# A decoder layer on one core: the third LayerNorm, the router and the transfers into expert order moved into the LSTM recurrence

## The reference

```
x = x + attention(layernorm(x))                       # 16 heads of 8, one shared K and V
x = x + xattn(layernorm(x), context)                  # two-layer LSTM with attention, 64 steps
x = x + ffn(layernorm(x))                             # eight experts, one per token

def step((h0, c0, h1, c1, a), x_t):                   # 64 times, each needs the one before
    h0, c0 = lstm([x_t, a], h0, c0);  h1, c1 = lstm(h0, h1, c1)
    p = softmax((h1 @ Wq.T) . context[b])             # over the 64 context rows of b
    a = tanh([p @ context[b], h1] @ Wo.T + bo);  return a

logits = x @ router_W + router_b                      # ffn, on x = layernorm(...)
gates = one_hot(argmax(softmax(logits))) * softmax(logits)
y = relu(x @ W1[e] + b1[e]) @ W2[e] + b2[e];  out = gates . y
```

## Time and profile before

| | us |
|---|---|
| median of 3 runs | 1802.16 (1801.74 to 1804.47) |
| profiled execution | 1804.93, span 1803.2 |
| TensorE busy | 1479.9 (82%), weight loads 1289.7 (72%) |
| VectorE busy | 1159.9 (64%) |
| ScalarE busy | 736.0 (41%) |
| POOL busy | 220.0 (12%) |

### The profile page before, as it was taken

How to read it: one execution, slowest core, us unless ns; L and a number is a source line. 1 busy time by engine, 2 the same in 40 slices (tenths; PEclk the granted TensorE clock), 3 DMA queues, 4 the chain that set the end, 5 groups by cost and what they waited for, 6 DMA issues and landing times. The chain is left out here.

```text
span 1803.2 us, 82779 instructions
## 1 busy us (share of the span) xinstructions
PE 1479.9 (82%) x34347; PEld 1289.7 (72%) x34348; DVE 1159.9 (64%) x4481; ACT 736.0 (41%) x1856; POOL 220.0 (12%) x427
## 2 busy tenths in 40 slices
PE   1547777777756999999999999999999968249997
PEld 0436666666645888888888888888888858237665
DVE  5878888888875666565656566666666658425454
ACT  2436666665643344444434343434443422013332
POOL 0000000000000000000000000000000003743333
PEclk9868988888966999999999999999999975569999
DMA  6000000000030000000000000000000036322221
GB/s 222 1 1 1 0 0 0 0 0 0 0 84 12 1 0 0 0 0 0 0 0 0 0 0 0 0 0 0 0 0 0 0 103 208 128 84 75 75 75 42
DMA packets 33458, 50.04 MB, mean 28 GB/s; under 512 B 4714, under 2 KB 24684, under 8 KB 32648
## 3 DMA queue, kind: packets, MB, share of 16 engines
q1 hardware_dynamic: 27312, 35.50, 6.7%
q0 software_dynamic: 5376, 12.66, 2.0%
q10 hardware_dynamic: 728, 1.34, 0.2%
HBM read 30.52 MB, written 19.48 MB: 28 GB/s over the span
## 5 line engine op out<-in xcount | busy, mean ns | idle before, releaser
L1554 DVE TENSOR_TENSOR hb<-psH,b_sb 128x512 f32<-128x512 f32 x72 | 49.8, 692 | 118.4 <-PE psH L1349 118.4
L891 PE MATMUL sc_a<-h_a,KH 128*128 128x48 f16 (+2 forms) x4096 | 123.9, 183 | 2.5 <-DVE h_a L1045 2.5
L891 PE MATMUL sc_b<-h_b,KH 128*128 128x48 f16 (+2 forms) x4096 | 122.9, 183 | 0.0
L851 PE MATMUL z_a<-h_a,WL 128*128 128x64 f16 x2304 | 112.5, 193 | 9.3 <-DVE h_a L1037 1.9
L851 PE MATMUL z_b<-h_b,WL 128*128 128x64 f16 x2304 | 111.9, 193 | 8.4 <-DVE h_b L1037 0.6
L931 PEld LDWEIGHTS mx_b<-pmv_b,VH 128*128 128x128 f16 x4096 | 107.1, 96 | 16.4 <-DVE pmv_b L1073 16.4
L931 PEld LDWEIGHTS mx_a<-pmv_a,VH 128*128 128x128 f16 x4096 | 107.1, 96 | 16.2 <-DVE pmv_a L1073 16.2
L931 PE MATMUL mx_b<-pmv_b,VH 128*128 128x16 f16 x4096 | 113.0, 169 | 5.4 <-DVE pmv_b L1073 0.4
L931 PE MATMUL mx_a<-pmv_a,VH 128*128 128x16 f16 x4096 | 113.0, 169 | 5.2 <-DVE pmv_a L1073 0.4
L891 PEld LDWEIGHTS sc_a<-h_a,KH 128*128 128x128 f16 x4096 | 112.8, 96 | 2.8 <-DVE h_a L1045 2.6
L466 PE MATMUL psK<-ident,xn 128*128 128x128 f32 x64 | 20.9, 327 | 113.2 <-DVE VB L671 86.6
(11 more groups left out here) (291 smaller groups left out, 3556.6 us busy)
## 6 DMA issues: line engine op xcount, KB each, us to landing
xr<-sorted_x SPq DMA_DIRECT2D x72, 129.0 KB, 2.1
XT<-in_ctxT SPq DMA_DIRECT2D x1, 4096.0 KB, 13.2
x_scratch<-X SPq DMA_DIRECT2D x1, 4096.0 KB, 15.9
TOK<-x_scratch SPq DMA_DIRECT2D x4, 1024.0 KB, 10.6
sorted_x<-zt SPq DMA_DIRECT2D x16, 129.0 KB, 6.4
w_sb<-in_w SPq DMA_DIRECT2D x1, 2048.0 KB, 10.3
b_sb<-in_b SPq DMA_DIRECT2D x1, 2048.0 KB, 21.1
out<-ys,xr POOLq DMA_INDIRECT x72, 2.3
```

The source lines that it names most:

```text
L851: mm = nc.tensor.matmul(q.z[layer][:, j * GB:(j + 1) * GB], WL[:, blk + j, w, :], mov[m], start=False, stop=False, skip_group_check=True)
L891: mm = nc.tensor.matmul(A.S[:, WIDE * n:WIDE * n + streamed(n)], KH[:, k, pair * P:(pair + 1) * P], A.h[1][:, 2 * n:2 * n + streamed(n) // ...
L1554: nc.vector.tensor_tensor(hb[:, u, :], psH[:, u, :], b1_sb[:, bass.ds(col, FF)], ALU.add).then_inc(v_hb, 1)
```

## The change

The hand-over up to `tables` is taken out of block 5 and put into block 4, one token tile per step, as a pipeline of which each stage runs a step or half a step behind the one before. n is the tile, t the step; `odd` is the group whose attention part runs in this half (0: a, 1: b).
- Half 0 of step t: TensorE transposes a of tile t-1 (both groups, now side by side in `A32`) and does `routing` (logits of t-3, ranks of t-4); VectorE normalises t-2, makes the gate of t-4 and adds x1 of t-1; ScalarE copies logits and ranks; POOL copies the normalised x of t-2 and the row numbers into `TOK`.
- Half 1: TensorE transposes the normalised x of t-2; VectorE does the statistics of t-1 and the maximum of the logits of t-3; ScalarE copies the transposed x and does the exponential; POOL does `place` of t-4, `rstd` of t-1 (a reciprocal root by three rounds of Newton), `choose` of t-3, and the indirect transfer of t-4.
- Four steps T to T+3 without recurrence drain the pipeline; then one matmul gives the totals and `tables` runs.
- ScalarE, POOL and VectorE loop over four steps a turn, and eight first and four last steps are written out.
- The two groups share one bank for the scores and one for the mixture; the two banks that this frees, `psE` and `psF`, carry the new matmuls.
- x1 comes by one load per tile; W1 and W2 are loaded into `X`, b1 beside it, all during the recurrence. The copies of a32 to X go. In the diff below the order is TensorE, VectorE, ScalarE, POOL; `place` and `choose` are 5 and 7 instructions of one to eight columns, written like those of `rstd`. Block 5 loads only b2 and runs the tile loop, which is unchanged.

```diff
-                q.a32 = sb(f"a32_{t}", [P, GB])
+                q.a32 = A32[:, g * GB:(g + 1) * GB]
-                q.S = ps("sc")
-                q.M = ps("mx")
+                q.S = psS
+                q.M = psM
...
+            def run_steps(eng, first_half, step, turn):
+                first_half()
+                for t in range(HEAD):
+                    step(t, t % SLOTS)
+                with eng.Fori(HEAD, T - TAIL - turn + 1, turn) as t:
+                    for k in range(turn):
+                        step(t + k, (HEAD + k) % SLOTS)
+                for t in range(T - TAIL, T + 4):
+                    step(t, t % SLOTS)
...
+                    def turn_a(n):
+                        pe.wait_ge(G[0].s_ta, n + 1)
+                        pe.wait_ge(G[1].s_ta, n + 1)
+                        wait(pe, a_xt, n - 1)
+                        nc.tensor.transpose(psE[:, 0:P], A32[:, :], ident[:, :]).then_inc(p_e1, 1)
+                    def turn_xn(n):
+                        pe.wait_ge(v_xn, n + 1)
+                        pe.wait_ge(v_x2, n + 2) if live(n + 1) else None
+                        nc.tensor.transpose(psE[:, 0:P], XN[:, :], ident[:, :]).then_inc(p_e2, 1)
+                    def routing(t):
+                        if live(t - 3):
+                            pe.wait_ge(a_xt, t - 2)
+                        if live(t - 4):
+                            pe.wait_ge(g_one, t - 3)
+                            wait(pe, g_acc, t - 4)
+                        wait(pe, a_lr, t - 3)
+                        if live(t - 3):
+                            nc.tensor.matmul(psF[:, 0:NE], xT[:, :], rw_sb[:, :], start=True, stop=False)
+                            mm = nc.tensor.matmul(psF[:, 0:NE], ones[0:NE, :], rbd[:, :], start=False, stop=True)
+                        if live(t - 4):
+                            nc.tensor.matmul(psF[:, NE:2 * NE], upper[:, :], one[:, :], start=True, stop=False)
+                            mm = nc.tensor.matmul(psF[:, NE:2 * NE], ones16[:, :], acc[:, :], start=False, stop=True)
...
                             if not last:
                                 early1(A)
+                        if odd == 0 and live(t - 1):
+                            turn_a(t - 1)
+                        if odd == 1 and live(t - 2):
+                            turn_xn(t - 2)
...
+                        if odd == 0:
+                            routing(t)
+                        if A:
                             pe.wait_ge(A.s_pm, 2 * at + 2)
...
+                        if odd == 0:
+                            if live(t - 2):
+                                normalise(t - 2, (m - 2) % SLOTS)
+                            if live(t - 4):
+                                gate(t - 4, (m - 4) % SLOTS)
+                        if odd == 1:
+                            if live(t - 1):
+                                statistics(t - 1, (m - 1) % SLOTS)
+                            if live(t - 3):
+                                best(t - 3)
                         if A:
                             dve.wait_ge(A.s_sc, at + 1)
...
+                        if odd == 0 and live(t - 1):
+                            add_x1(t - 1, (m - 1) % SLOTS)
...
+                        if odd == 1 and live(t - 2):
+                            act.wait_ge(p_e2, t - 1)
+                            wait(act, p_lr, t - 2)
+                            nc.scalar.activation(xT[:, :], psE[:, 0:P], ACT.Copy).then_inc(a_xt, 1)
+                        if odd == 1 and live(t - 3):
+                            act.wait_ge(v_nm, t - 2)
+                            nc.scalar.activation(eg[:, :], lr[:, 0, :], ACT.Exp, bias=nm[:, 0:1],
+                                                 accum_out=sm[:, 0:1]).then_inc(a_eg, 1)
...
+                    def after(n):
+                        pool.wait_ge(g_r, n)
+                        pool.sem_inc(g_go, 1)
+                    def rstd(n):
+                        ready(v_ag, n + 1)
+                        ready(v_xn, n)
+                        k = 11 * n
+                        pool.tensor_scalar(ve[:, :], mv[:, 1:2], EPS, None, ALU.add).then_inc(g_r, 1)
+                        after(k + 1)
+                        pool.tensor_scalar(yr[:, :].bitcast(I32), ve[:, :].bitcast(I32), -0.5, 1597463007.0,
+                                           ALU.mult, ALU.add).then_inc(g_r, 1)
+                        pool.tensor_scalar(vh[:, :], ve[:, :], -0.5, None, ALU.mult).then_inc(g_r, 1)
+                        for i in range(3):
+                            after(k + 3 * i + 3)
+                            pool.tensor_tensor(yu[:, :], yr[:, :], yr[:, :], ALU.mult).then_inc(g_r, 1)
+                            after(k + 3 * i + 4)
+                            pool.tensor_scalar(yu[:, :], yu[:, :], vh[:, 0:1], 1.5, ALU.mult, ALU.add).then_inc(g_r, 1)
+                            after(k + 3 * i + 5)
+                            if i < 2:
+                                pool.tensor_tensor(yr[:, :], yr[:, :], yu[:, :], ALU.mult).then_inc(g_r, 1)
+                            else:
+                                pool.tensor_tensor(rs[:, :], yr[:, :], yu[:, :], ALU.mult).then_inc(g_rs, 1)
...
+                        if odd == 0 and live(t - 2):
+                            copy_xn(t - 2, (m - 2) % SLOTS)
+                        if odd == 1:
+                            if live(t - 4):
+                                place(t - 4, (m - 4) % SLOTS)
+                            if live(t - 1):
+                                rstd(t - 1)
+                            if live(t - 3):
+                                choose(t - 3)
+                            if live(t - 4):
+                                scatter(t - 4, (m - 4) % SLOTS)
-                            pool.tensor_copy(X[:, bass.ds(at * B + A.g * GB, GB)], A.a32[:, :]).then_inc(A.s_ao, 1)
```

More of the change, by code:

```diff
@@ new lines, in decoder_kernel @@
+            z2 = sb("z2", [P, 2])
+            z1 = sb("z1", [P, 1])
+            one = sb("one", [P, NE], F16)
+            acc = sb("acc", [P, NE], F16)
+            w8 = sb("w8", [P, NE])
+            w4 = sb("w4", [P, 4])
+            w2s = sb("w2s", [P, 2])
+            slot = sb("slot", [P, SLOTS], U32)
+            zt = sb("zt", [P, ROW])
+            base = sb("base", [P, NE])
+            first = sb("first", [P, NE])
+            cnt = sb("cnt", [P, NE])
+            cnti = sb("cnti", [P, NE], I32)
@@ new lines, in decoder_kernel @@
+            unit = sb("unit", [P, NE])
+            end = sb("end", [P, NE])
+            tilestart = sb("tilestart", [P, NT])
+            past = sb("past", [P, NT, NE])
+            tex = sb("tex", [P, NT])
+            rowf = sb("rowf", [P, NT])
+            lasti = sb("lasti", [P, NE], I32)
+            d_x1 = [sem(f"d_x1{u}") for u in range(SLOTS)]
+            d_sc = [sem(f"d_sc{u}") for u in range(SLOTS)]
+            d_rw = sem("d_rw")
+            d_w = sem("d_w")
+            d_z = sem("d_z")
@@ new lines, in decoder_kernel, with live @@
+            a_lr = sem("a_lr")
+            a_eg = sem("a_eg4")
+            g_c = sem("g_c4")
+            g_go = sem("g_go4")
+            g_r = sem("g_r")
+            g_rs = sem("g_rs")
+            g_xn = sem("g_xn")
+            g_pl = sem("g_pl")
+            g_acc = sem("g_acc")
+            g_one = sem("g_one")
+            g_ch = sem("g_ch")
+            def live(n):
+                return not isinstance(n, int) or 0 <= n < T
+            def run_steps(eng, first_half, step, turn):
[7 more added lines that the diff above has]
+                    step(t, t % SLOTS)
@@ new lines, in run_halves, with step @@
+            def run_halves(half, eng, turn):
+                def step(t, m):
+                    if not isinstance(t, int) or t < T - 1:
+                        half(G[1], G[0], t, t, t, m)
+                        half(G[0], G[1], t + 1, t, t, m)
+                    elif t == T - 1:
+                        half(G[1], G[0], t, t, t, m)
+                        half(None, G[1], None, t, t, m)
+                    else:
+                        half(None, None, None, None, t, m, 0)
+                        half(None, None, None, None, t, m, 1)
+                run_steps(eng, lambda: half(G[0], None, 0, None, None, None, None), step, turn)
@@ L939, in _, with half @@
                         early1(q)
-                    run_halves(half, pe)
+                    run_halves(half, pe, 1)
+                    pe.wait_ge(g_acc, T)
+                    pe.wait_ge(a_lr, T + 1)
+                    nc.tensor.matmul(psF[:, 0:NE], ones16[:, :], acc[:, :], start=True, stop=True).then_inc(p_lr, 1)
                 @block.scalar
                 def _(act):
-                    def half(L, A, lt, at):
+                    def half(L, A, lt, at, t, m, odd=-1):
+                        odd = A.g if A else odd
                         def gate_tanh(l):
@@ new lines, in half @@
```

(16 more changed lines are left out.)

508 lines of the change are left out of this document (211 added, 297 removed).

## The result

The changed kernel takes 1898.7 us (median of four runs, 1896.3 to 1968.1) against 1803.1 before: ratio 1.0529, interval 1.0511 to 1.0547. It is slower by 96 us. The forecast was 1742 us. The run of 1968.1 had a granted clock of 0.63 throughout, so the profile shown here is that of a later run of 1899.5 us. It belongs to a group of runs in which the kernel before takes 1823.3 and the changed one 1903.8, ratio 1.0431 (1.0375 to 1.0488).

The account below looks back on a forecast made before the run. TensorE, hardly resting, was taken to bound the recurrence, and POOL's work the hand-over. 1804.93 - 89.6 (hand-over) + 27 (steps) + 3 (start) = 1745.3, less 2.8 for the runs' median: 1742.5 us, range 1715 to 1795.

Parts of the forecast that it names:

- What comes into each step: Part of the prediction pricing the work added to each recurrence step, engine by engine: 0.42 us a step, 27 us over 64.
- `add_x1` (an operation like `sm`, 0.29) lies in the 0.42 ahead of `pmv`: VectorE in the recurrence step: the added 0.29 us operation fits in the 0.42 us VectorE waits before `pmv`.
- without a wait for pmv: Sign in the half with `routing`: weight loads of `mx` start about 0.3 us later after WO's, with no wait for `pmv`.
- POOL as the bound: POOL in the recurrence step: bound only above 0.44 us an instruction; over 0.5 was included in a rival of chance 0.12.
- 24 x 0.28 ... = 10.1 of 13.9: POOL in the recurrence step: 24 small instructions at 0.28 us, copies and a scatter take 10.1 of 13.9 us.
- The hand-over: Between recurrence and tile loop: 128.8 us goes, 39.2 stands in its place, so 89.6 us is given back.
- The start: Before TensorE's first matmul: some twenty small POOL instructions and the router weights' load add 2 to 4 us, taken as 3.
- The shared banks: PSUM banks of scores and mixture, shared by both groups in the recurrence: no wait is added, 0.
- The sum on TensorE: Recurrence step: TensorE gets 0.70 us more work, 0.30 of it on the path for `routing`; all additions together 0.42.
- Rival 1: Recurrence step: TensorE absorbs nothing, all 0.70 us added plus 0.15 of late `sm`, 54 us in all, 1769.5 us; chance 0.20.
- rival 2: Recurrence step: everything hides but 0.1 us a step, 6 us in place of 27, 1721.5 us; chance 0.08.
- Rival 3: Recurrence: POOL's activity stretches VectorE's two-SBUF-input operations, deciding from 0.93 us a step; 1838 us at three per half; chance 0.12.

Follow-up runs that it names:

- eight-slot kernel: The changed kernel with eight TOK slots and eight trailing steps (SLOTS and TAIL 8 in place of 4): 1783.3 us, ratio 0.9783.
- early scatter: The changed kernel with the scatter of tile t-4 issued right behind `place`, ahead of `rstd` and `choose`, four slots: 1812.4 us, ratio 0.9925.
- one-round kernel: The changed kernel with one Newton round in `rstd` in place of three: 1806.9 us, ratio 0.9900.
- early-scatter kernels with turns of four: Changed kernel, scatter right behind `place`, loops of four steps: alone 1812.4 us; with one Newton round 1810.2; with that and routing matmuls issued twice 1856.5.
- gated kernel with one round: Changed kernel, scatter behind `place` but held until VectorE has made group b's masked scores, one Newton round in place of three: 1779.9 us, ratio 0.9875.

## Why the prediction was wrong

**The step that failed** is in "What comes into each step", VectorE: "`add_x1` (an operation like `sm`, 0.29) lies in the 0.42 ahead of `pmv`". Its length was counted and fits; its wait was not. It waits for the landing of the scatter four tiles back, and the order of the stages puts that scatter last in POOL's half, a few us ahead of the `add_x1` that needs its slot. The prediction named waits for `rs` and for `one`, and never the one from a transfer to the buffer it reads. Of its own signs, "without a wait for pmv" is the one that failed. Eight slots take 120 us away, an earlier scatter 91 (1903.8 to 1812.4 us, by step 1.47 x 63 = 93). None of the three rivals had it; the nearest, POOL as the bound, was held to be far off.

**POOL's size** made it bite. "24 x 0.28 ... = 10.1 of 13.9": measured 0.37 to 0.41 from start to start, 0.45 to 0.55 behind a two-operation one; place 1.6, rstd 4.9, choose 3.1, scatter 2.5, copies 1.2: 13.3 us. It is no bound by its sum yet, but in the eight-slot kernel it rests only 1.4 us of a step, and in the ring of four slots rstd, choose and the scatter stood in series. Either error alone would have been cheap. At 0.28 for each of the 18 spacings from `ve` to `one` the same ring would be 17.06 - 7.83 + 5.04 = 14.3 us (an estimate), no longer than the step that was forecast; and with eight slots the measured sizes leave the ordinary step at 14.30. The memset and select of the earlier trace rows were the nearest rows but depend on each other by one wait; the new instructions take a wait and a second semaphore step each. The upper end, 0.5, was used for the range's tail only and not for the step, where it gives 24 x 0.5 + 3.4 = 15.4 us: that should have been a rival of its own with more than a share of 0.12.

**What was right.** The hand-over (-82 for -89.6; 6 of the miss is the tail of four steps: 53 instructions at 0.39, 53 x 0.11 = 6). The start, as far as the traces resolve it (+2.2 for +3). The shared banks (0 for 0). The sum on TensorE in its size: the ordinary step of the eight-slot kernel is 14.30, +0.37, where the sum had 0.42. Its terms are not shown one by one, and some luck is in it: routing takes 0.71 from its first load to the first of the mixing product, not 0.49, and fills a hole of 0.25, which by itself would be 0.46. Rival 1 (+0.85) falls with the sum, rival 2 (+0.1) too. Rival 3 falls: the operations of the recurrence that VectorE had before take 9.94 us a step in the changed kernel and 10.10 with eight slots, against 9.79. That is +0.15 and +0.31, where rival 3 needed 0.93 on the path.

**What was missing beside.** Three costs of the step are in no part of the prediction: the stretches of half clock (51 us in the eight-slot kernel's recurrence, 15 of them at 1.3 us: 20 us), the loop turns (four steps a turn were held to save branches; eight cost 3.4 us a turn), and the results of TensorE that come late beside a scatter, about 0.9 us a step with the early scatter. The changed kernel has these too, 21 gate tanhs by 0.3 to 0.7 us, but there the ring covers them.

## What to carry over

When stages are folded into a loop, write down for each buffer the ring from its last reader, a transfer's landing included, back to its next writer, and compare the ring's sum with the step: a wait that costs an idle engine nothing stands here in front of the whole critical chain. Work that is hidden has a place as well as a size; moving one GpSimd transfer forward by a few us was worth 91 us, and left it in a place that cost 0.9 us a step. Price small dependent instructions by pairs that have the same waits as the new ones, or carry the upper bound into the step.

## What was not expected of the hardware

A result of TensorE reaches VectorE and ScalarE late beside a GpSimd indirect scatter. In the traces of all kernels with the scatter in the loop, 226 times a last scores matmul ended 0 to 1.3 us after a scatter's start; in 219 of them the masked scores began over 0.3 us late, in all but one of these 1.3 to 1.6 us after the scatter's start. The other `sm` began 0.04 us after their matmul, save behind a late `XN` or a turn of the loop. Waits of VectorE and ScalarE for each other in the same stretch were served in 0.03 us (184 of 184), and instructions of both ran through it.

It is the signal that is late and not TensorE's stream. In the one-round kernel and in the early-scatter kernels with turns of four the semaphore update that releases the late ones is itself recorded 0.86 to 0.92 us (medians) after the matmul's end, against 0.014 otherwise, and `sm` follows it by 0.02 us in either case. Behind the late ones TensorE goes on loading weights at its usual pace: the fourteenth load ends 0.48 us after the start of the last scores matmul, late or not. The ends of matmuls in a trace are modelled (the Trainium skill, page Perfetto Trace Analysis, section Summary: the profiler window per engine type, calls them estimated), so whether the write to PSUM or only the update is held back stays open. Nowhere else does it occur: over all these traces and their waits of VectorE and ScalarE for TensorE, each of the 384 updates that came over 0.3 us after the matmul's end belongs to a matmul that ended within 1.3 us of a scatter's start, and the kernel before, with no scatter in its loop, has none.

The Trainium skill, page SBUF — State Buffer, section Who interferes with whom, says that TensorE and ScalarE never wait on anyone and that VectorE contends with GpSimd only with certain SBUF inputs or modes. The trace agrees as to TensorE's own loads, which go on; the lateness of its signal is something else, and it holds up VectorE and ScalarE all the same.

Open is why it depends on the place. In the gated kernel with one round 119 of 119 results of TensorE that ended beside a scatter were on time, in the eight-slot kernel 88 of 92. There they are those of layer-1 gates and a transpose, ahead of which TensorE has short waits of its own, while the late `sm` end dense runs. But in the changed kernel 21 of 38 layer-1 gate results with the same short waits were late, so that is not the whole of it, and it was not tried by itself.

The granted clock of TensorE was 1.00 in the recurrence of the kernel before up to its last 2 us, busy 388.6 of 400. With the change it falls to half in stretches in every variant, 41 to 194 us in all, and a stretch costs 1.3 us in a step that is otherwise full. In the changed kernel most of them follow the wait for the landing; in the eight-slot kernel 12 of the 16 had no wait of TensorE over 0.15 us in the 10 us ahead of them, and what sets those off no run shows.

The version to keep of those run is the one with eight slots, 1783.3 us: ratio 0.9783 to the kernel before in its group, some 0.99 where the old hand-over takes 128.8 us.
